# Sixteen sends of rows, two slots apart in GpSimd's order instead of one

## The chip, the cores and the metric

The kernel runs on one core of a Trainium2 chip. The metric is the device time of one execution in microseconds. The time before is the median of three runs, 1697.31 us (1696.88 to 1698.7). The engines are named as the profile names them: PE is TensorE, DVE is VectorE, ACT is ScalarE, POOL is GpSimd, and SP is SyncE, which only issues DMAs here. They run side by side, each through its own instructions in a fixed order, and they meet at semaphores.

## The reference

`x` has the shape 16 x 256 x 512, and so has the context. Four residual steps follow one another; the dimensions are those of the data.

```
x = x + xattn0(layernorm(x), ctx)   # latent attention, norm over the latent, relu, out_w
x = x + ffn0(layernorm(x))          # dense layer plus 2 of 8 low-rank experts per row
x = x + xattn1(layernorm(x), ctx)   # 8 heads, 512 x 512 scores each
x = x + ffn1(layernorm(x))          # 64 experts, top 8 of each row, inner size 192

xattn0: h = relu((t_x - mean) * rsqrt(var + eps) * ln_gamma + ln_beta); out_w @ h + out_b + ctx
ffn1:   probs = softmax(logits); topw, topi = top_k(probs, 8); topw /= sum(topw)
        an expert takes at most CAP rows of each group of 1024, in order of rows
```

Each of the 4096 rows goes to up to eight experts. A row beyond an expert's capacity is dropped for that expert.

## The kernel before, in words

**Stages.** The attention stage works through the 16 batches of 256 rows. It ends with every normalised row copied to the slots of its experts in `slots_dram`, a table in HBM. Then the expert stage reads these slots expert by expert, and the last part merges what two sets of outputs hold.

**Slots.** The attention stage's order is written out by `schedule` (L87). Its unit is the slot, a quarter of a head's 512 x 512 scores: PE multiplies (L691 and L700), DVE takes a maximum (L1209), ACT takes the exponential (L973, `p_t`). A batch has 32 slots. Its preparation (both earlier residual steps) begins 64 slots ahead, and its routing (the `disp` events) follows behind, so at any time several batches are in work. The tables (TENSOR, SCALAR, VECTOR, GPSIMD and their _OUT, _TAIL and _MAX companions) give each step its slot on each engine, and an engine runs its steps sorted by slot. No engine looks at another's order. A step whose input isn't there holds up all that follows on its engine.

**What POOL does per batch.** Counted by the batch's 32 slots, POOL has these steps:

- `add` (L1479): eight sums `p_sum` of two `p_t` tiles, at slots 5 to 8 and 21 to 24. Each needs ACT's `p_t`, and PE sums the result in L727.
- `lat_rstd` (L1451, L1453) at slot 25: the root for the latent norm of a later batch. It waits for DVE's `lat_all` (L1121). DVE's L1126 waits for it, then L1130, then ACT's relu (L917), then PE's `out_w` product (L642).
- `rstd2`, `rstd4` and `rstd` (L1408 to L1416): roots and offsets of the other norms.
- `res0` and `res1` (L1446): the residual additions of the context.
- the dispatch `rstd` (L1408, L1410), at slot 14.25 of the next batch: the root for the rows that are sent.
- `send`, 16 per batch (L1491), from slot 31 of the next batch but one: an indirect DMA that scatters 128 rows of 577 values by the expert slots in `slot_i`. The first waits for `slots_ok`, DVE's last routing step of that batch (L1307), and all wait for the slots to have been filled once with defaults. Each counts up `sent`; DVE's writing of rows two batches later (L1248) waits for that count.

**The lines behind it.** PE's L663 and L656 are the low-rank products of ffn0, read by DVE's `lora_mid` (L1149); L620 is a product of the latent attention, which waits for ACT's `prob` (L907); L723 turns the maxima, read by ACT's `max_hi` (L980) and DVE's `max_lo` (L1218); L753 is the router's product, read by DVE's `r_max` (L1255); L798 is the expert stage's first product.

**The end of the attention stage.** Behind the last batch's additions stand, in POOL's order, the 16 sends of batch 13, then batch 15's dispatch `rstd`, then the 32 sends of batches 14 and 15. The expert stage's first reads (`x_slots<-slot_rows`) wait for all sends.

Of the kernel before, what the change touches and what calls it, by code (L numbers as in the profile page):

```python
# [32 lines left out]
class Count:  # L33
# [5 lines left out]
    def up(self, by=1):  # L39
# [25 lines left out]
SCALAR_OUT = {"x0": 38.25, "x1": 40.25, "exp": 42.5}  # L65
VECTOR_OUT = {"stats0": 10.25, "stats1": 12.75, "rows0": 16.5, "rows1": 17.75, "peak": 42.25, "top0": 43.75,
              "top1": 43.75, "top2": 43.75, "place0": 44.5, "place1": 44.5, "place2": 46.5}
GPSIMD_OUT = {"rstd": 14.25, "send": 63}
SYNC_OUT = {"out": 10}

TENSOR_TAIL = {"sums0": -4, "sums2": -3.5, "sums1": 0.25}
# [15 lines left out]
def schedule(dims, prepare, tail, maxima, dispatch, core):  # L87

    B, HALF, NHEAD, C = dims["B"], dims["HALF"], dims["NHEAD"], dims["T"] // P
    H4 = NHEAD // HALF
    QUAD, SLOTS = C * H4, NHEAD * C
    AHEAD = LEAD * H4
    out = []
    if "fill" in core:
        late = dims["NEXP"] - FIRST_FILLS
        out += [(prepare["k0"] - PREPARE, 0, ("fill", n)) for n in range(FIRST_FILLS)]
        out += [(FILL_FROM + n * FILL_SLOTS / late - PREPARE, 0, ("fill", FIRST_FILLS + n)) for n in range(late)]
    for n in range(B * SLOTS):  # L100
        if "key" in core:
            out.append((n, 0, ("key", n)))
        if "score" in core:
            out.append((n - AHEAD, 1, ("score", n)))
        if "add" in core and n // H4 % C == 1:
            out.append((n + 1, 2, ("add", n)))
        if "weighted" in core and n % H4 == 0:
            out.append((n + WEIGHTED, 2, ("pv", n // H4)))
    for quad in range(B * HALF):
        out += [(QUAD * (quad + 1) - AHEAD - 1 + o, 3, ("tail", quad, what)) for what, o in maxima.items()]  # L110
        out += [(QUAD * (quad + 1) + o, 3, ("tail", quad, what)) for what, o in tail.items()]
    for b in range(B):
        out += [(SLOTS * b - PREPARE + o, 4, ("prep", b, what)) for what, o in prepare.items()]
        for what, o in dispatch.items():
            for n in range(HALF * dims["TOPK"] if what == "send" else 1):
                out.append((SLOTS * (b + 1) + o + n, 5, ("disp", b, what, n)))
    return [(at, ev) for at, _, ev in sorted(out, key=lambda x: x[:2])]


# [20 lines left out]
def build(nc, a, out, out_odd, slots_dram, dims):  # L140
# [22 lines left out]
    BC = NHEAD * C  # L163

    tensor_order = schedule(dims, TENSOR, TENSOR_TAIL, TENSOR_MAX, TENSOR_OUT, ("key", "score", "weighted"))
    scalar_order = schedule(dims, SCALAR, SCALAR_TAIL, SCALAR_MAX, SCALAR_OUT, ("key",))
    vector_order = schedule(dims, VECTOR, VECTOR_TAIL, VECTOR_MAX, VECTOR_OUT, ("score",))
    gpsimd_order = schedule(dims, GPSIMD, {}, {}, GPSIMD_OUT, ("add",))
    sync_order = schedule(dims, SYNC, {}, SYNC_MAX, SYNC_OUT, ("fill",))
# [1428 lines left out]
```

## Time and profile before

| | before |
|---|---|
| median of 3 runs | 1697.31 us |
| profiled execution: span, first to last instruction | 1788.0 us |
| PE busy | 1562.6 us (87%) |
| DVE busy | 1256.5 us (70%) |
| ACT busy | 971.5 us (54%) |
| POOL busy | 807.0 us (45%) |
| sends, L1491 | 256 in POOL, 255.0 us busy |
| additions, L1479 | 128, 168.5 us busy |
| mean granted PE clock | 0.935 |

The profiled execution is one execution with the recording on, and its span is the only time that the profile gives of it; it gives none for what lies around the span. It is 90.7 us above the median of the runs, which were taken without recording. The attention stage fills the span up to 1231.43 us, where PE begins the first expert (L798). The sends stand in it from 289.2 to 1226 us. A share of busy time is an average: in a steady batch PE is nearly always busy, and at the end of the stage POOL alone is.

### The profile page before, as it was taken

What the parts mean: (1) busy time and instruction counts of PE and PEld (TensorE: products, weight loads), DVE (VectorE), ACT (ScalarE), POOL (GpSimd) and SP (SyncE); (2) the same over time, 40 slices, a digit from 0 to 9 for tenths busy, and PEclk for the clock granted to TensorE, in tenths of its full rate; (3) what the DMA queues carried; (4) which work ended last, traced back from release to release, by engine and by line L of the source; (5) the groups of instructions that cost most, each with busy time, mean ns of one, the idle gap of its engine ahead of it and who ended that gap; (6) DMA issues with size and microseconds to landing.
All of it is one profiled execution on the core that took longest, in us unless ns stands there. A gap on an engine that the chain in (4) does not pass through costs nothing.

```text
span 1788.0 us, 25255 instructions
## 1 busy us (share of the span) xinstructions
PE 1562.6 (87%) x8016; PEld 999.9 (56%) x8016; DVE 1256.5 (70%) x2994; ACT 971.5 (54%) x1938; POOL 807.0 (45%) x893
## 2 busy tenths in 40 slices
PE   5799999999999999999899898724999999999980
PEld 2444454454444454444444443324999999999970
DVE  2477778767767677687677676434888888888850
ACT  3355665655655655655656544412666666666640
POOL 4122325454463554464454535654444444444440
PEclk8889999999999999999999998956999999999995
DMA  9968863463463444433422422025999999999969
GB/s 328 309 196 298 270 206 113 132 206 106 132 186 121 128 132 127 135 102 99 134 75 79 113 53 57 23 96 181 287 291 297 297 290 295 297 299 288 296 104 188
DMA packets 156099, 329.22 MB, mean 184 GB/s; under 512 B 28010, under 2 KB 38122, under 8 KB 154944
## 3 DMA queue, kind: packets, MB, share of 16 engines
q1 hardware_dynamic: 115968, 247.80, 42.4%
q0 software_dynamic: 40000, 79.82, 20.4%
q8 instruction: 64, 1.05, 0.2%
q14 instruction: 67, 0.55, 0.1%
HBM read 149.64 MB, written 173.21 MB: 181 GB/s over the span
## 4 chain that ended last, share of the span: by engine, by line
PE 69%; DVE 9%; another core or an unknown queue 5%; issue 4%; SPq 4%; ACT 3%; POOL 2%; DMA 2%; DVEq 1%; POOLq 0%; ACTq 0%
PE bank L700 7%; PE bank L712 6%; PE bank L691 5%; PE bank L809 5%; PE bank L811 5%; PE bank L810 5%; PE bank L798 3%; PE bank L669 3%; PE bank L734 3%; PE bank L614 2%; SPq L492 2%; DVE max_col L1209 2%; PE bank L620 2%; PE bank L832 2%
## 5 line engine op out<-in xcount | busy, mean ns | idle before, releaser
L1209 DVE TENSOR_REDUCE max_col<-bank 128x1 f32<-128x512 f32 x512 | 341.0, 683 | 173.4 <-PE bank L691 155.8
L973 ACT ACTIVATE p_t<-bank 128x512 f32<-128x512 f32 x512 | 294.4, 596 | 217.1 <-PE bank L700 195.3
L1491 POOL DMA_INDIRECT slot_rows<-row,slot_i x256 | 255.0, 996 | 77.6 <-issue 76.9
L700 PE MATMUL bank<-q_stack,k_stack 98*128 98x512 f32 x512 | 278.5, 546 | 8.3 <-DMA q_stack<-max_lo 4.2
L1479 POOL TENSOR_TENSOR p_sum<-p_t 128x512 f32<-128x512 f32 x128 | 168.5, 1322 | 214.1 <-ACT p_t L973 211.5
L691 PE MATMUL bank<-k_stack,q_stack 96*128 96x512 f32 x512 | 214.1, 420 | 4.7 <-DVE max_col L1209 4.4
L700 PEld LDWEIGHTS bank<-q_stack,k_stack 98*128 98x128 f32 x512 | 98.5, 193 | 196.4 <-issue 170.1
L809 PE MATMUL bank<-gate_up_hi,x_slots_t_hi 128*128 128x384 f32 x512 | 183.4, 358 | 0.5 <-DVE x_slots_t_lo L1337 0.5
L1533 POOL DMA_INDIRECT out_rows<-y_slots,row_ids x64 | 110.0, 1719 | 153.9 <-ACT y_slots L1045 150.7
L811 PE MATMUL bank<-gate_up_hi,x_slots_t_lo 128*128 128x384 f32 x512 | 172.4, 337 | 0.0
L810 PE MATMUL bank<-gate_up_lo,x_slots_t_hi 128*128 128x384 f32 x512 | 172.0, 336 | 0.0
L1533 POOL DMA_INDIRECT out_rows_odd<-y_slots,row_ids x64 | 109.6, 1713 | 132.1 <-ACT y_slots L1045 127.9
L712 PE MATMUL bank<-p_t,v_t 128*32 128x512 f32 x1024 | 143.3, 633 | 0.2 <-DVE head_sb L1225 0.2
L1045 ACT ACTIVATE y_slots<-bank,x_slots 128x512 f32<-128x512 f32 x128 | 88.2, 689 | 100.6 <-PE bank L836 100.6
L669 PE MATMUL bank<-base_w,x_t 128*128 128x512 f32 x256 | 132.0, 630 | 0.0
L691 PEld LDWEIGHTS bank<-k_stack,q_stack 96*128 96x128 f32 x512 | 99.9, 195 | 52.8 <-issue 29.1
L1337 DVE TENSOR_TENSOR x_slots_t_lo<-bank,x_slots_t_hi 128x512 fp32r<-128x512 f32 x128 | 88.0, 688 | 54.7 <-ACT x_slots_t_hi L1025 39.5
L1362 DVE TENSOR_TENSOR gate_up_lo<-gate_up,gate_up_hi 128x768 fp32r<-128x768 f32 x128 | 121.7, 951 | 0.0
L1055 ACT CAST gate_up_hi<-gate_up 128x768 fp32r<-128x768 f32 x128 | 105.5, 825 | 10.8 <-DMA gate_up<-in_gate_up 10.8
L798 PE MATMUL bank<-ident,x_slots 128*128 128x128 f32 x512 | 77.4, 274 | 38.3 <-DMA x_slots<-slot_rows 38.3
L1408 POOL TENSOR_SCALAR row_rstd<-row_mv 128x2 f32<-128x2 f32 x48 | 11.0, 228 | 205.2 <-DVE row_mv L1095 205.2
L809 PEld LDWEIGHTS bank<-gate_up_hi,x_slots_t_hi 128*128 128x128 f32 x512 | 96.9, 189 | 1.1 <-DVE x_slots_t_lo L1337 0.9
(188 smaller groups left out, 3296.4 us busy)
## 6 DMA issues: line engine op xcount, KB each, us to landing
gate_up<-in_gate_up SPq DMA_DIRECT2D x64, 768.0 KB
slot_rows<-row SPq DMA_DIRECT2D x64, 577.0 KB, 8.2
x_slots<-slot_rows SPq DMA_DIRECT2D x64, 577.0 KB, 5.7
k_stack<-prob SPq DMA_DIRECT2D x192, 128.0 KB, 3.8
down<-in_down SPq DMA_DIRECT2D x64, 384.0 KB, 8.9
q_stack<-x_t SPq DMA_DIRECT2D x128, 128.0 KB
out_rows_odd<-row SPq DMA_DIRECT2D x17, 512.0 KB, 5.5
x<-in_x SPq DMA_DIRECT2D x16, 512.0 KB, 3.3
```

Of the source, the lines that this page charges most:

```text
L669: e.matmul(bank[:, :], x_t[:, k, c, :], base_w[:, c, :], start=c == 0, stop=False)
L691: e.matmul(psum[2 + n % 2][:, :], q_st[b % 2][0:SK, head, c * P:(c + 1) * P], k_st[b % 2][0:SK, head, :], start=True, stop=True).then_inc( ...
L700: e.matmul(psum[n % 2][:, :], k_st[b % 2][0:SKM, head, j * P:(j + 1) * P], q_st[b % 2][0:SKM, head, :], start=True, stop=True).then_inc(fu ...
L712: m = e.matmul(psum[4][h * DQ:(h + 1) * DQ, :], v_t[b % 2][:, j, head + h, :], p_t[step % 2][:, h, :], start=j == 0, stop=j == C - 1)
L809: e.matmul(bk[:, 0:2 * INNER], xt_hi[u % 3][:, c, :], gu_hi[nw][:, c, :], start=c == 0, stop=False)
L810: e.matmul(bk[:, 0:2 * INNER], xt_hi[u % 3][:, c, :], gu_lo[nw][:, c, :], start=False, stop=False)
L811: m = e.matmul(bk[:, 0:2 * INNER], xt_lo[u % 3][:, c, :], gu_hi[nw][:, c, :], start=False, stop=c == C - 1)
L973: e.activation(p_t[step % 2][:, h, :], psum[n % 2][:, :], ACT.Exp, scale=SCALE).then_inc(free[n % 2], 1)
L1209: e.tensor_reduce(max_col[quad % 2][:, h, c:c + 1], psum[2 + n % 2][:, :], X, ALU.max, negate=True).then_inc(free[2 + n % 2], 1)
L1479: e.tensor_tensor(p_sum[:, h, :], p_t[(step - 1) % 2][:, h, :], p_t[step % 2][:, h, :], ALU.add).then_inc(p_sum_ok, 1)
L1491: e.indirect_dma_start(out=slots_dram, in_=rows[b % 2][:, k, :], in_offset=None, out_offset=bass.IndirectOffsetOnAxis(ap=slot_i[b % 2][:, ...
L1533: e.indirect_dma_start(out=out_odd if e_ % 2 else out, out_offset=bass.IndirectOffsetOnAxis(ap=row_ids[e_ % NI][:, q, :].bitcast(U32), axi ...
```

## The change

The first send of a batch moves from slot 63 of the dispatch table to slot 48, and the 16 sends stand two slots apart. The last stays where it was: 63 + 15 = 48 + 2 x 15 = 78. Counted by the 32 slots of a batch, the sends of batch b stood at 31 of batch b+2 and 0 to 14 of batch b+3; now they stand at 16, 18, ... 30 and 0, 2, ... 14. Nothing else is changed. The orders of PE, DVE, ACT and SP are the same as before, and so are the semaphores and their counts.

```diff
-GPSIMD_OUT = {"rstd": 14.25, "send": 63}
+GPSIMD_OUT = {"rstd": 14.25, "send": 48}
+SEND_STEP = 2
...
             for n in range(HALF * dims["TOPK"] if what == "send" else 1):
-                out.append((SLOTS * (b + 1) + o + n, 5, ("disp", b, what, n)))
+                out.append((SLOTS * (b + 1) + o + n * SEND_STEP, 5, ("disp", b, what, n)))
```

Line numbers behind the new line are one higher after: the send is L1491 before and L1492 after.

POOL in a steady batch, from slot 21 on, before. `p_sum` is the addition, `lat_all` is `lat_rstd`, `row_rstd` and `row_off` here are `rstd2`, `slot_rows` is a send:

```order
L1479 TENSOR_TENSOR p_sum<-p_t 128x512 x4
L1451 TENSOR_SCALAR lat_all<-lat_all 128x1
L1453 TENSOR_TENSOR lat_all<-lat_all,neg_half 128x1
L1408 TENSOR_SCALAR row_rstd<-row_mv 128x2
L1410 TENSOR_TENSOR row_rstd<-row_rstd,neg_half 128x2
L1414 TENSOR_TENSOR row_off<-row_mv,row_rstd 128x2
L1416 TENSOR_SCALAR row_off<-row_off 128x2
```

POOL at the same place after. Three sends and two additions stand where the four additions began:

```order
L1492 DMA slot_rows<-row,slot_i 16384x577 x3
L1480 TENSOR_TENSOR p_sum<-p_t 128x512 x2
L1492 DMA slot_rows<-row,slot_i 16384x577
L1480 TENSOR_TENSOR p_sum<-p_t 128x512 x2
L1492 DMA slot_rows<-row,slot_i 16384x577
L1452 TENSOR_SCALAR lat_all<-lat_all 128x1
L1454 TENSOR_TENSOR lat_all<-lat_all,neg_half 128x1
L1492 DMA slot_rows<-row,slot_i 16384x577 x2
L1409 TENSOR_SCALAR row_rstd<-row_mv 128x2
```

Three sends (slots 16, 18 and 20) now stand ahead of the additions of slots 21 to 24, one stands in the middle of these four and one between the last of them and `lat_rstd`, and two (slots 26 and 28) stand between `lat_rstd` and `rstd2`.

POOL at the end of the attention stage before, from the last four additions on. The 16 sends are batch 13's, the 32 are those of batches 14 and 15, and `row_rstd` is batch 15's dispatch `rstd`:

```order
L1479 TENSOR_TENSOR p_sum<-p_t 128x512 x4
L1491 DMA slot_rows<-row,slot_i 16384x577 x16
L1408 TENSOR_SCALAR row_rstd<-row_mv 128x2
L1410 TENSOR_TENSOR row_rstd<-row_rstd,neg_half 128x2
L1491 DMA slot_rows<-row,slot_i 16384x577 x32
```

POOL there after:

```order
L1492 DMA slot_rows<-row,slot_i 16384x577 x3
L1480 TENSOR_TENSOR p_sum<-p_t 128x512 x2
L1492 DMA slot_rows<-row,slot_i 16384x577
L1480 TENSOR_TENSOR p_sum<-p_t 128x512 x2
L1492 DMA slot_rows<-row,slot_i 16384x577 x12
L1409 TENSOR_SCALAR row_rstd<-row_mv 128x2
L1411 TENSOR_TENSOR row_rstd<-row_rstd,neg_half 128x2
L1492 DMA slot_rows<-row,slot_i 16384x577 x32
```

Four sends moved from behind the four last additions to places ahead of and between them; the 32 at the end are as before.

## Rows read from the trace of the kernel before

**Rows 1.** The page: span; the chain that ended last, by engine.
```profile
span 1788.0 us, 25255 instructions
...
PE 69%; DVE 9%; another core or an unknown queue 5%; issue 4%; SPq 4%; ACT 3%; POOL 2%; DMA 2%; DVEq 1%; POOLq 0%; ACTq 0%
```

**Rows 2.** Windows: A:B, us, then each engine's busy time (instructions), PEclk, DMA share, GB/s.
```profile
215.10:277.50 62.40, 62.06 (x318) 31.78 (x318) 50.23 (x128) 40.46 (x82) 19.12 (x27) 1.00 0.63 198
...
343.60:1039.20 695.60, 647.20 (x3170) 328.59 (x3170) 509.73 (x1271) 403.86 (x811) 351.32 (x421) 0.97 0.40 121
```

**Rows 3.** Waits of PE, 290 to 1130 us: total us, times, longest.
```profile
PE bank L663 <- DVE gated L1187: 26.3, 12, 3.8
...
PE bank L620 <- ACT prob L907: 25.8, 11, 3.0
```

**Rows 4.** Waits of ACT, 290 to 1130 us.
```profile
ACT max_hi L980 <- remote: 33.1, 11, 3.6
```

**Rows 5.** Timeline, 946 to 950 us: start, us, engine, line, operation, [idle before <-releaser].
```profile
946.35 0.28 PE L723 MATMUL bank<-ident,max_col 128*16 128x128 f32 x1
...
946.38 0.97 POOL L1491 DMA_INDIRECT slot_rows<-row,slot_i  x1 [0.30 <-issue]
...
948.97 0.25 ACT L980 CAST max_hi<-bank 16x128 fp32r<-16x128 f32 x1 [2.68 <-remote]
```

**Rows 6.** Chain of waits, 1140 to 1240 us: start, us, what.
```profile
1162.96 12.79 another core or an unknown queue
```

**Rows 7.** All sends, line L1491: duration min/median/max in ns.
```profile
L1491 POOL DMA_INDIRECT slot_rows<-row,slot_i x256: 967/973/1371, 289.2 to 1225.2; - x128
```

**Rows 8.** L1451 (lat_rstd) on POOL: ns min/median/max, first and last; what it waited for.
```profile
L1451 POOL TENSOR_SCALAR lat_all<-lat_all x16: 185/190/192, 31.2 to 1040.8; 128x1 f32<-128x1 f32 x16
...
  DVE lat_all L1121: 45.0, 16
```

**Rows 9.** Timeline of POOL, 894 to 909 us.
```profile
894.26 2.62 POOL L1479 TENSOR_TENSOR p_sum<-p_t 128x512 f32<-128x512 f32 x2 [10.60 <-ACT p_t L973]
...
897.21 2.60 POOL L1479 TENSOR_TENSOR p_sum<-p_t 128x512 f32<-128x512 f32 x2 [0.32 <-ACT p_t L973]
...
900.43 0.19 POOL L1451 TENSOR_SCALAR lat_all<-lat_all 128x1 f32<-128x1 f32 x1 [0.63 <-DVE lat_all L1121]
...
900.71 0.56 POOL L1453 TENSOR_TENSOR lat_all<-lat_all,neg_half 128x1 f32<-128x1 f32 x1
...
908.38 0.22 POOL L1408 TENSOR_SCALAR row_rstd<-row_mv 128x2 f32<-128x2 f32 x1 [7.11 <-DVE row_mv L1095]
```

**Rows 10.** Timeline of DVE, `slots_ok` of the batch that is sent next.
```profile
885.08 0.17 DVE L1307 TENSOR_SCALAR slot_i<-slot 128x16 int32<-128x16 f32 x1
```

**Rows 11.** Timeline of DVE, ACT and PE, 901 to 906 us.
```profile
901.46 0.74 DVE L1126 SCALAR_TENSOR_TENSOR theta<-theta,lat_all,ln_gamma 128x512 f32<-128x512 f32 x1
...
903.02 0.63 ACT L917 ACTIVATE theta<-theta 128x512 f32<-128x512 f32 x1
...
903.86 1.98 PE L642 MATMUL bank<-theta,out_w 128*128 128x512 f32 x4
```

**Rows 12.** Timeline of POOL, a send between two additions, 1122 to 1125 us.
```profile
1122.85 0.99 POOL L1491 DMA_INDIRECT slot_rows<-row,slot_i  x1 [0.16 <-issue]
...
1123.86 1.30 POOL L1479 TENSOR_TENSOR p_sum<-p_t 128x512 f32<-128x512 f32 x1
```

**Rows 13.** Timeline of POOL, last additions to last sends, 1147 to 1184 us.
```profile
1147.66 4.99 POOL L1479 TENSOR_TENSOR p_sum<-p_t 128x512 f32<-128x512 f32 x4 [7.65 <-ACT p_t L973]
...
1172.07 0.97 POOL L1491 DMA_INDIRECT slot_rows<-row,slot_i  x1 [0.30 <-issue]
...
1181.38 0.22 POOL L1408 TENSOR_SCALAR row_rstd<-row_mv 128x2 f32<-128x2 f32 x1 [8.33 <-DVE row_mv L1095]
...
1183.17 1.29 POOL L1491 DMA_INDIRECT slot_rows<-row,slot_i  x1 [0.76 <-DVE slot_i L1307]
```

**Rows 14.** Timeline of DVE, the last routing step.
```profile
1175.78 0.29 DVE L1255 TENSOR_REDUCE r_max<-bank 128x2 f32<-128x128 f32 x1 [12.82 <-remote]
```

## The prediction

> **What bounds the kernel now.** I read the page first, with the times beside it. The span is 1788.0 us [rows 1], and the median of the runs is 1697.31 us: the recorded execution is 90.7 us longer. Then I read where the chain of waits goes. PE has 69% of it, and 5%, some 89 us, is put down to "another core or an unknown queue" [rows 1]. There is no other core here, so the reader should see time for which no instruction of the kernel accounts. The windows tell where it lies. A batch before the first send takes 62.40 us, of which PE is busy 62.06. Ten batches with sends take 695.60 us, 69.56 each, with 64.72 busy [rows 2]. The 7.16 us per batch are what such waits make: in 12 batches PE waits 26.3 us for `gated` and 25.8 us for `prob` [rows 3], and ACT's `max_hi` sits 33.1 us behind nothing that is shown, 11 times [rows 4]. One of these: PE's L723 has begun at 946.35 and takes 0.28 us, ACT's L980, which waits for it alone, begins at 948.97, 2.68 us idle, while sends run back to back from 946.38 [rows 5]. The largest is 12.79 us, in the run of 16 sends at the end [rows 6].
>
> Two readings are possible: the sends hold up the signals between engines in every execution, or only while a record is taken. By the first, the runs of 1697.31 us contain the 89 us; by the second they don't. I take the second, because of a sum. The excess of the recorded execution over the timed ones (90.7) is the size of the unexplained part of the chain (89); if the timed runs contained it too, the 90.7 us would need another source, and I found none. With the stalls gone, a batch of the timed run is the 62.4 us of the first window: PE is busy for 99% of it, and any delay that PE meets stays. That holds from about 215 to 1130 us. From there on POOL is the bound: its sends follow one another and the expert stage waits for the last.
>
> The Trainium skill bears on this ("NOTIFIC — the notification-queue block", 7.1 Overflow): the path that carries records pushes back inside rather than lose one. By that rule the recording can throttle an engine, and the gaps here would be its doing; the page gives no time for it. The trace agrees as far as a gap of 2.68 us stands under back-to-back sends, but cannot prove it.
>
> **The change, part by part.** It adds and removes no instruction; 256 sends of 973 ns (median; 967 to 1371) stay [rows 7]. Only their places in POOL's order move. All is worked out for the batch at 894 us. There are 12 like it: `lat_rstd` stands in batches -2 to 13 by POOL's order, 64 slots ahead of its own, the sends stand in batches 2 to 17, and 2 to 13 have both.
>
> *Three sends ahead of the additions* (slots 16, 18, 20). They wait for `slots_ok`, here 885.08 + 0.17 = 885.25 [rows 10]. Three sends at a pitch of 1.28 us (0.97 + 0.30) end at 889.1. The additions begin at 894.26 after 10.60 us of idleness [rows 9]. The idle time hides them: nothing, with 5.2 us to spare; were `slots_ok` that much late, additions and PE's L727 would be late by the rest.
>
> *Two sends among the additions and `lat_rstd`* (22 and 24). This is the term that decides. Before, the additions are 894.26 + 2.62 = 896.88, then 897.21 + 2.60 = 899.81 with an idle 0.32, and `lat_rstd` begins at 900.43, 0.63 us after POOL is free, when DVE's value is there [rows 9]. It waits for DVE in all 16 batches, 45.0 us together [rows 8], and the last of them is at 1040.8 us. It ends at 900.71 + 0.56 = 901.27, and DVE's L1126 begins at 901.46 [rows 11]: 0.19 us of slack. A send between two additions costs 1.17 us (1122.85, next addition 1123.86, and 0.16 idle before) [rows 12]. So after: additions to 896.88, send to 898.05, additions to 900.65, send to 901.82, `lat_rstd` until 902.66. L1126 then begins 1.2 us late. Behind it on DVE stand L1130, `max_col` and all else. ACT's relu stood at 903.02, 0.63 long, and PE's L642 at 903.86 [rows 11], 0.21 us behind it. So PE is held 1.0 to 1.2 us. PE is at 99% in such a batch [rows 2], so no later idleness takes this up: 12 x 1.1 = 13 us. Bounds: 0 if DVE catches up before PE needs it; 12 x 1.5 = 18 if neither the 0.32 us of idleness between the additions nor the 0.19 us of slack is there without recording.
>
> *Two sends behind `lat_rstd`* (26, 28). They end by 902.66 + 2.6 = 905.3; `rstd2` begins at 908.38 after 7.11 us of idleness [rows 9]. Hidden, with 3 us to spare.
>
> *The other nine* (30, and 0 to 14 by twos). Before, all 16 stood in slots 31 to 14; there are fewer now, so `rstd4`, the residual additions and the additions of slots 5 to 8 come no later. Gain: nothing in a steady batch, because PE doesn't wait for these in the first window either. Bounds: 0 to -0.3 us a batch.
>
> *The end.* Four of batch 13's 16 sends go from behind the last additions to before and between them. Before, the four additions run from 1147.66 to 1152.65 and the sends until 1172.07 + 0.97 = 1173.04. Then the dispatch `rstd` waited 8.33 us for DVE, until 1181.38, and the 32 sends begin at 1183.17 [rows 13]. DVE was late by the 12.79 us of rows 6: its `r_max` began only at 1175.78 [rows 14], 5.60 us ahead of `rstd`. Without the stall DVE would allow `rstd` at 1181.38 - 12.79 = 1168.6, and POOL is the bound, until 1173.04. After, three sends (3.8 us) fit into the 7.65 us of idleness ahead of the additions [rows 13], one among them costs 1.17, and 12 follow: 1152.65 + 1.17 + 12 x 1.28 = 1169.2. That is 3.8 us sooner and close to what DVE allows. I take -3, bounds -4 and 0 (if DVE's chain is late for another reason). In the two groups of additions before these a send costs or gives at most 1.5 us; I take 0.
>
> Sum: 13 - 3 = 10 us. Its terms are from the profiled execution, cleared of the stalls; since the runs are taken to be without them, it is added to their median: 1697.31 + 10 = 1707 us. The span of the recorded execution is a different sum: of its 89 us of stalls most would go, because sends in runs of four and fewer take the place of runs of six to eight, so it should fall: 1788 - 0.8 x 89 + 13 = 1730 us or a little more, although the time rises.
>
> **Rivals.**
>
> *A, the stalls are in the timed runs too.* Then spreading the sends removes most of 7.16 us in ten batches, say nine tenths, 65 us, less the 13 of `lat_rstd`: 52 us faster, 1645 us. For it speaks that the gaps stand exactly where sends are dense; against it, the 90.7 us that the recorded execution is longer. Chance 0.12.
>
> *B, DVE's delay doesn't reach PE.* For it: DVE is busy only 50.23 of 62.40 us [rows 2], so it recovers within microseconds. Against it: the relu's end (903.02 + 0.63) and L642 are 0.21 us apart [rows 11], so PE is there before DVE has recovered. Then the sum is between -3 and +3, within 1697.3 +- 3.4. Two tenths of a per cent, 3.4 us, is about what a measurement of this kernel can tell from no change. Chance 0.11.
>
> *C, the delay costs more than itself.* DVE's `max_col` behind L1126 frees PE's banks; 1.2 us late there and 1.2 us late at relu might add instead of overlap, as both engines restart behind PE: up to 12 x 1.8 = 22 less 3, 1716 us. For it: DVE waits for PE's L691 and PE for DVE's `max_col` by turns in every slot; against it, the banks give them a slot or more of play. Chance 0.17.
>
> *D, the order doesn't matter in the timed run*, because without stalls ACT's `p_t` comes sooner than in the trace and POOL's work slides apart. The slack of `lat_rstd` is the same in all batches, so I give it no more than 0.02, inside B's time.
>
> **How the numbers follow.** Forecast 0.58 (1701 to 1713), A 0.12, B and D 0.13, C 0.17. The predicted time is the likeliest, 1707. The range leaves out A, which lies 45 us off, and little else: 1693 to 1716. Slower by over 0.2%: forecast and C, 0.75. Within: 0.11 of B and D. Faster: A and the edge of B, 0.14.
>
> **What would show it.** In the profile after, POOL's `lat_all` L1452 should no longer wait for DVE in those 12 batches, and DVE's L1127 should wait for POOL 1.2 us in 12 batches, PE's L643 for ACT's relu 1 us. The "unknown queue" share should drop under 2%, with a span of 1730 to 1740. Batch 15's dispatch `rstd` should wait for POOL's sends less than before. The forecast is wrong if the time falls with the span (A), or if DVE's L1127 waits 12 times and PE doesn't (B).

## The result, and the profile after

| | before | after |
|---|---|---|
| median, measured side by side, 12 runs each | 1698.09 us (1694.62 to 1705.42) | 1706.51 us (1704.65 to 1708.6) |
| ratio, 95% interval | | 1.0046 [1.0034, 1.0058] |
| profiled execution: span | 1788.0 us | 1703.0 us |
| mean granted PE clock | 0.935 | 0.955 |
| POOL busy | 807.0 us | 819.6 us |

The changed kernel is 8.4 us slower. Its profiled execution took 1705.14 us, so 2.1 us lie around its span. That is within the range of its timed runs; the 1788.0 us of the kernel before lie far above the range of its own.

The page of the changed kernel, its span and the chain by engine, is the counterpart of [rows 1]:

```profile
span 1703.0 us, 25255 instructions
...
PE 33%; POOL 2%; issue 2%; DVE 2%; DMA 1%; ACT 1%; POOLq 0%; DVEq 0%; SPq 0%; ACTq 0%
```

The "unknown queue" is gone from the chain. The first window (columns as in [rows 2]) holds ten batches with sends, the second one earlier batch, in which only the first three sends stand:

```profile
338.50:977.70 639.20, 620.60 (x3171) 317.86 (x3171) 510.64 (x1271) 406.57 (x811) 361.62 (x421) 1.00 0.44 130
...
212.10:274.60 62.50, 62.10 (x318) 31.83 (x318) 50.48 (x128) 40.54 (x82) 22.58 (x30) 1.00 0.67 213
```

A batch with sends takes 63.92 us, the one before them 62.50. The 69.56 us and the PE clock of 0.97 of [rows 2] don't come back. The 1.4 us more per batch show as two waits, PE's and then DVE's (total us, times, longest; 290 to 1130 us):

```profile
PE bank L724 <- DVE max_col L1210: 16.9, 11, 1.6
```

```profile
DVE theta L1127 <- POOL lat_all L1454: 9.8, 11, 0.9
```

Neither wait was there before. PE's two waits of [rows 3], for `gated` and `prob`, are gone (one of 0.6 us is left for `gated`). Before, POOL was free early at `lat_rstd` and waited for DVE's value in all 16 batches [rows 8]. Now it waits only in four:

```profile
L1452 POOL TENSOR_SCALAR lat_all<-lat_all x16: 185/188/193, 31.0 to 980.9; 128x1 f32<-128x1 f32 x16
...
  DVE lat_all L1122: 35.9, 4
```

One batch on POOL, the counterpart of [rows 9]. The send that was put between the additions, and the one behind them:

```profile
845.15 2.62 POOL L1480 TENSOR_TENSOR p_sum<-p_t 128x512 f32<-128x512 f32 x2 [3.28 <-ACT p_t L974]
847.92 1.27 POOL L1492 DMA_INDIRECT slot_rows<-row,slot_i  x1
849.21 2.52 POOL L1480 TENSOR_TENSOR p_sum<-p_t 128x512 f32<-128x512 f32 x2
851.89 0.99 POOL L1492 DMA_INDIRECT slot_rows<-row,slot_i  x1 [0.17 <-issue]
852.96 0.19 POOL L1452 TENSOR_SCALAR lat_all<-lat_all 128x1 f32<-128x1 f32 x1
853.23 0.58 POOL L1454 TENSOR_TENSOR lat_all<-lat_all,neg_half 128x1 f32<-128x1 f32 x1
```

`lat_rstd` comes 0.1 us behind a send, with no idle time. DVE, ACT and PE there (before: [rows 11]), from PE's L635 on, from whose result DVE makes its value:

```profile
849.79 0.38 PE L635 MATMUL bank<-lat_mv,ones 128*128 128x2 f32 x2 [0.32 <-DVE lat_mv L1118]
...
851.01 0.74 DVE L1122 SCALAR_TENSOR_TENSOR lat_all<-lat_all 128x1 f32<-128x1 f32 x1
...
853.84 0.75 DVE L1127 SCALAR_TENSOR_TENSOR theta<-theta,lat_all,ln_gamma 128x512 f32<-128x512 f32 x1 [0.89 <-POOL lat_all L1454]
...
855.42 0.63 ACT L918 ACTIVATE theta<-theta 128x512 f32<-128x512 f32 x1 [1.41 <-DVE theta L1131]
...
856.13 0.27 PE L724 MATMUL bank<-ident,max_col 128*16 128x128 f32 x1 [1.56 <-DVE max_col L1210]
```

Read them in time. L1127 waits 0.89 us for POOL, ACT's relu waits 1.41 for DVE, and PE's L724, which stands ahead of L643, waits 1.56 us for the `max_col` that DVE does behind L1131. The row 851.01 is a second matter: L1122 took 0.22 us in the kernel before, in the row that follows, and takes 0.74 here.

```profile
900.13 0.22 DVE L1121 SCALAR_TENSOR_TENSOR lat_all<-lat_all 128x1 f32<-128x1 f32 x1
```

The end on POOL (before: [rows 13]), from the first of the 12 sends behind the last additions to the first of the 32:

```profile
1080.01 0.99 POOL L1492 DMA_INDIRECT slot_rows<-row,slot_i  x1 [0.17 <-issue]
...
1094.11 0.98 POOL L1492 DMA_INDIRECT slot_rows<-row,slot_i  x1 [0.30 <-issue]
...
1096.39 0.22 POOL L1409 TENSOR_SCALAR row_rstd<-row_mv 128x2 f32<-128x2 f32 x1 [1.30 <-DVE row_mv L1096]
...
1098.19 1.29 POOL L1492 DMA_INDIRECT slot_rows<-row,slot_i  x1 [0.75 <-DVE slot_i L1308]
```

The 12 sends take 15.1 us, and `rstd` then waits 1.30 us for DVE where it waited 8.33. PE's first product of the experts:

```profile
1146.55 1.94 PE L799 MATMUL bank<-ident,x_slots 128*128 128x128 f32 x8 [38.41 <-DMA x_slots<-slot_rows]
```

The span ends 556.5 us behind it, as before (1231.43 + 556.6). So the whole difference of the spans lies ahead of the experts.

### The profile page after: what moved, and what is told of

Its sections match the earlier page's. It is cut to its first block and busy times, and to the rows that moved or that the text cites. A ratio compares the mean times of both kernels' runs of the same rounds, so it can differ in the third digit from the quotient of the medians.

```text
span 1703.0 us, 25255 instructions
## 1 busy us (share of the span) xinstructions
PE 1525.4 (90%) x8016; PEld 983.2 (58%) x8016; DVE 1258.4 (74%) x2994; ACT 974.0 (57%) x1938; POOL 819.6 (48%) x893
## 5 line engine op out<-in xcount | busy, mean ns | idle before, releaser
L1492 POOL DMA_INDIRECT slot_rows<-row,slot_i x256 | 266.6, 1041 | 104.0 <-issue 68.6
L713 PE MATMUL bank<-p_t,v_t 128*32 128x512 f32 x1024 | 137.2, 608 | 0.2 <-DVE head_sb L1226 0.2
L670 PE MATMUL bank<-base_w,x_t 128*128 128x512 f32 x256 | 124.6, 599 | 0.0
L811 PEld LDWEIGHTS bank<-gate_up_lo,x_slots_t_hi 128*128 128x128 f32 x512 | 97.1, 190 | 0.0
```

Of the source, the lines that this page charges most:

```text
L713: m = e.matmul(psum[4][h * DQ:(h + 1) * DQ, :], v_t[b % 2][:, j, head + h, :], p_t[step % 2][:, h, :], start=j == 0, stop=j == C - 1)
L811: e.matmul(bk[:, 0:2 * INNER], xt_hi[u % 3][:, c, :], gu_lo[nw][:, c, :], start=False, stop=False)
L1492: e.indirect_dma_start(out=slots_dram, in_=rows[b % 2][:, k, :], in_offset=None, out_offset=bass.IndirectOffsetOnAxis(ap=slot_i[b % 2][:, ...
```

## The experiments

The kernel before ran beside each group, and it took 1794.63, 1793.4, 1772.14 and 1785.38 us in these four, not 1698. So in these groups its timed runs are as long as its first profile was. The groups ran on chips 8, 4, 12 and 12; which chip the first measurement used isn't known. The kernels are therefore compared within a group, or by the length of a batch in their profiles. That length is here the distance from the fifth to the last of DVE's 16 `lat_stat` (L1115 before), divided by 11.

| kernel | time, us | ratio to the kernel before | batch, us | last `lat_stat` to first expert, us |
|---|---|---|---|---|
| before, first profile | (1698.09) | | 69.25 | 193.1 |
| after, first profile | (1706.51) | 1.0046 | 63.92 | 169.8 |
| e1 before again | 1792.41 | 0.9994 [0.9964, 1.0025] | 69.29 | 194.1 |
| e2 `lat_rstd` ahead | 1708.48 | 0.9523 [0.9493, 0.9553] | 63.17 | 180.8 |
| e3 steady only | 1726.12 | 0.9617 [0.9591, 0.9643] | 64.18 | 184.6 |
| e4 tail only | 1792.35 | 0.9983 [0.9953, 1.0014] | 69.28 | 191.9 |
| e5 after again | 1724.26 | 0.9626 [0.9595, 0.9657] | 64.22 | 179.6 |
| e6 none among | 1710.85 | 0.9550 [0.9520, 0.9580] | 62.66 | 181.0 |
| e7 one ahead | 1712.68 | 0.9673 [0.9588, 0.9758] | 63.15 | 179.9 |
| e8 old tail | 1710.12 | 0.9674 [0.9586, 0.9762] | 62.64 | 184.1 |
| e9 run of six | 1721.88 | 0.9733 [0.9648, 0.9818] | 63.70 | 182.7 |
| e10 half rows | 1793.36 | 1.0145 [1.0056, 1.0235] | 69.47 | 189.6 |
| e11 paced | 1740.01 | 0.9728 [0.9684, 0.9772] | 64.45 | 193.4 |
| e12 none among again | 1709.54 | 0.9571 [0.9525, 0.9617] | 62.71 | 180.6 |

Groups: e1 to e4, e5 and e6, e7 to e10, e11 and e12. Each profile is one execution. In what follows, a stall is time in which an engine sits idle though the profile shows nothing that it still waits for ("remote" or "another core or an unknown queue").

**e1, the kernel before once more** (no edit).

> The kernel before, unchanged, recorded once more. Theory (the stalls belong to the recording): time within 0.2% of the kernel before; if this recorded execution again has stalls, its span is up to 90 us above its timed runs and its batches with sends take 66 to 72 us; if it has none, its span is about 2 us under its time and its batches are constant, 62.4 to 63.0 us long. Rival (the stalls are in every execution): the batches take about 69.6 us and the timed runs sum up to that.

```profile
span 1792.0 us, 25255 instructions
...
PE 69%; DVE 9%; another core or an unknown queue 4%; issue 4%; SPq 4%; ACT 3%; POOL 2%; DMA 2%; ACTq 0%; POOLq 0%; DVEq 0%
```

Its time is that of the kernel before in the same group, 1794.63, but 94 us above the 1698.09 of the first measurement. Its ACT waits as [rows 4] shows, here over the whole span:

```profile
ACT max_hi L980 <- remote: 27.7, 10, 3.9
```

The span of each timed run here is some 2.1 us under its time, so timed runs are this long too, not only the profile. That doesn't settle the prediction's question. Every one of these timed runs, and of the kernel before in all four groups, carries a span and a clock, so something was recorded in each. Leaving out one of 2261.82 us, they take 1758 to 1805 us. Its 12 runs of the first measurement, for which no span is listed, take 1695 to 1705. So the two readings, stalls only under recording and stalls in some measurements, are not told apart by this kernel. The changed kernel adds one thing: its first profile is a recorded execution, with 12 and 32 sends in a row at its end, and shows no stall, where every other profile here has some at its end. Recording alone is then not enough. Whether it is needed, and whether the chip matters, is open.

**e5, the changed kernel once more** (no edit).

> The changed kernel once more, beside the kernel before on the same chip. If the chip makes the difference, the kernel before takes either 1698 or 1794 us here. Theory (dense sends stall the other engines only in some executions, and spaced sends don't): the changed kernel takes 1705 to 1715 us in both cases; so it is 8 us slower where the kernel before takes 1698, and 85 us faster where it takes 1794. Rival (everything is slower on such a chip): it takes 1790 us or more there.

The changed kernel takes 1724.26 us where the kernel before takes 1793.4: 69 us faster, 3.7%. Of the 18 us over the first measurement, 3.3 are in the batches (11 x 0.3, 64.22 against 63.92), 4.9 lie ahead of the fifth `lat_stat`, where no send stands yet, and 9.8 at the end, where 12 and 32 sends still stand in a row: 179.6 against 169.8 us. One piece of its chain of waits there:

```profile
1098.53 2.88 another core or an unknown queue
```

So one kernel pair gives two results: 8 us slower in the first measurement, and 69 us faster in a group where runs of sends stall the others.

**e2, `lat_rstd` ahead of the second send.**

```diff
-GPSIMD = {..., "lat_rstd": 25, ...}
+GPSIMD = {..., "lat_rstd": 24, ...}
```

> The changed kernel with lat_rstd at slot 24 instead of 25, so that it stands behind the addition of slot 24 and ahead of the send of slot 24; all sends stay two slots apart. Theory (the loss is lat_rstd held up by two sends): one of the two is out of its way, DVE's wait for lat_all falls from 0.9 us a batch to about 0 to 0.2, PE's wait at L724 from 1.5 to 0.3 us or less, the batch from 63.9 to 62.5 us or so, the time to 1689 to 1693 us, under the kernel before. Rival (the loss comes from the send between the additions or from elsewhere): 1705 us as after. Rival (only one send's 1.2 us is recovered, but PE waits for max_col anyway): 1698 us.

The batch falls from 64.18 us (e3, same group, same steady part as the changed kernel) to 63.17: 1.0 us, not the 1.4 of the theory. DVE's wait for `lat_all` is gone but for one batch. PE's wait at L724 is a third of what it was, and longer than the 0.3 us a batch expected:

```profile
PE bank L724 <- DVE max_col L1210: 5.0, 9, 0.6
```

What is left is in DVE's row 848.72. L1122 is still stretched to 0.74 us, because the send between the additions has pushed the last addition over it, and PE waits 0.55:

```profile
848.72 0.74 DVE L1122 SCALAR_TENSOR_TENSOR lat_all<-lat_all 128x1 f32<-128x1 f32 x1
...
850.59 0.74 DVE L1127 SCALAR_TENSOR_TENSOR theta<-theta,lat_all,ln_gamma 128x512 f32<-128x512 f32 x1
...
852.86 0.27 PE L724 MATMUL bank<-ident,max_col 128*16 128x128 f32 x1 [0.55 <-DVE max_col L1210]
```

**e6 and e12, no send among the additions.**

```diff
-SEND_STEP = 2
+SENDS = (48, 49, 50, 51, 58, 59, 60, 62) + tuple(range(64, 80, 2))
...
-                out.append((SLOTS * (b + 1) + o + n * SEND_STEP, 5, ("disp", b, what, n)))
+                out.append((SLOTS * (b + 1) + o + (SENDS[n] - 48 if what == "send" else 0), 5, ("disp", b, what, n)))
```

> The changed kernel with other places for eight of its sends: none stands among the additions of slots 21 to 24 or ahead of lat_rstd behind them. Sends at 16, 17, 18, 19, 26, 27, 28, 30 and 0, 2, ... 14; never more than four in a row. Theory: DVE's wait for lat_all is 0, a batch takes 62.4 to 62.9 us, 1.1 to 1.5 less than in the changed kernel, the time is 13 to 17 us lower than the changed kernel's in the same call, about 1690. Rival (a run of four or a send behind the additions costs as much): within 3 us of the changed kernel.

> The kernel with none among the additions once more, beside the kernel before. Theory: 1705 to 1712 us where the kernel before takes 1770 to 1795; about 1690 where it takes 1698 (the changed kernel's 1706.5 less 12 x 1.3).

The batch is 62.66 us, 1.56 less than in e5, and the time 13.4 us less (1724.26 to 1710.85, one group). In the two profiles the spans are 17.2 apart (1721.5 and 1704.3): eleven batches at 1.56 make 17.2, and 1.4 more at the end are made up ahead of the fifth batch. The medians are 13.4 apart; the e6 profile is the fastest of its five runs. The window of ten batches, columns as in [rows 2]:

```profile
339.70:966.60 626.90, 621.98 (x3172) 318.62 (x3170) 505.43 (x1272) 405.19 (x811) 354.75 (x421) 1.00 0.45 132
```

PE is busy for 99.2% of them. The same edit again, e12, gives 1709.54 us. This version beats the kernel before in both groups and the changed one in the one that they share. It was not measured where the kernel before takes 1698 us, so that it would win there is not shown. The changed kernel's 1706.51 less 13.4 would be 1693 us there, an estimate.

The same places as in the profile after, in e6:

```profile
842.14 0.38 PE L635 MATMUL bank<-lat_mv,ones 128*128 128x2 f32 x2 [0.32 <-DVE lat_mv L1118]
...
843.36 0.22 DVE L1122 SCALAR_TENSOR_TENSOR lat_all<-lat_all 128x1 f32<-128x1 f32 x1
...
844.70 0.74 DVE L1127 SCALAR_TENSOR_TENSOR theta<-theta,lat_all,ln_gamma 128x512 f32<-128x512 f32 x1
```

L1127 begins 2.56 us behind L635; in the changed kernel it was 4.05. L1122's durations (min/median/max in ns) show the second price by itself. First before (there L1121):

```profile
L1121 DVE SCALAR_TENSOR_TENSOR lat_all<-lat_all x16: 219/219/221, 30.8 to 1040.5; 128x1 f32<-128x1 f32 x16
```

after:

```profile
L1122 DVE SCALAR_TENSOR_TENSOR lat_all<-lat_all x16: 219/741/750, 30.6 to 978.9; 128x1 f32<-128x1 f32 x16
```

and e6:

```profile
L1122 DVE SCALAR_TENSOR_TENSOR lat_all<-lat_all x16: 219/220/221, 29.9 to 968.7; 128x1 f32<-128x1 f32 x16
```

**e7, one send ahead of `lat_rstd`, none between the additions** (`SENDS` with 56 in place of 51).

> As the kernel with none among the additions (16 to 19, 26, 27, 28, 30, 0 to 14), but one send moves from slot 19 to slot 24, between the last addition of slots 21 to 24 and lat_rstd. Theory (lat_rstd has 0.63 us of idleness ahead and 0.19 us of slack behind it, and a send there costs 1.15 to 1.2): DVE's L1127 comes 0.35 us late, a batch takes 62.95 to 63.1 us against 62.65 there, the total is 4 to 5 us above that kernel. Rival (a send costs its full 1.2 us): 63.8 us a batch, +14. Rival (hidden): within 2.

DVE waits 0.37 us a batch, what is left of one send (1.17) after the 0.63 us of idleness and the 0.19 us of slack ahead of it:

```profile
DVE theta L1127 <- POOL lat_all L1454: 4.1, 11, 0.4
```

The batch is 63.15 us, 0.5 longer than e8's and e6's. The time was to be 4 to 5 us above e6's, which didn't run in this group; it is 2.6 above e8's. The send between the additions alone (e2) costs 0.5 too, and the pair 1.56: more than the two apart, since the slack can be used only once.

**e3 and e4, the steady batches and the end apart.** e3 sends as in the changed kernel up to batch 12 and as before from 13 on; e4 the other way round (`> 12`).

```diff
+def send_at(b, n):
+    return n * SEND_STEP if b <= 12 else 15 + n
...
```

> Batches 0 to 12 send as in the changed kernel, 13 to 15 as before. Theory: the whole loss of the steady batches stays and the end's gain goes: the kernel before + 12 x 1.1 to 1.5 = 1711 to 1716 us. If the end's gain is nothing, 1706 as after.

> Batches 0 to 12 send as before, 13 to 15 as in the changed kernel. Theory: only the end's gain: 3 us by the prediction, up to 8 by the difference between 12 batches x 1.5 us and the measured 8.4: 1690 to 1695 us. Rival (the end gains nothing, a steady batch loses 0.7 us): 1698 us. Together with the run that changes the steady batches alone the differences should sum to that of the whole change, +8.4 us.

The absolute forecasts of e2, e3 and e4 fell with the 1698 us they started from. e4 is inconclusive: 2.3 us under the kernel before, with an interval that holds zero. The two differences, 68.5 and 2.3 us, sum to 70.8, close to the 69 us of the whole change in e5. For the end the profiles tell more, with one execution each. In this group the changed end is 3.8 us shorter than the old one (e2 180.8, e3 184.6), and 2.2 shorter in the orders with long runs (e4 191.9, e1 194.1). e3 and e5, of two groups, differ only in the end: 5.0 us.

**e8, the old end under the version e6** (batches 13 to 15 send at slot 31 and 0 to 14).

> The kernel with none among the additions for batches 0 to 12, the sends of 13 to 15 as in the kernel before (slot 31 and 0 to 14). Theory: it costs what the changed end gains, 3 to 5 us by POOL's order (four sends of 1.28 us less behind the last additions), and by the stalls of a run of 16 in place of 12 perhaps 2 to 5 more where runs are stalled: 1713 to 1719 us. Rival (the end gains 10 us, the whole difference between 12 x 1.5 and the measured 8.4): 1720 or more.

The time is 3 us under the forecast, and within 1 us of e6's and e12's, which ran in other groups. In the profiles the end is 184.1 us, against 179.9 in e7 of the same group and 181.0 and 180.6 in e6 and e12: the changed end gains 3.1 to 4.2. All comparisons together give 2 to 5 us, and all of them have stalls in them.

**e9, six sends in a row in place of four** (the other line as in e6).

```diff
-SEND_STEP = 2
+SENDS = (48, 49, 50, 51, 58, 59, 60, 61, 62, 64, 66, 67, 68, 74, 76, 78)
```

> The kernel with none among the additions, with six sends in a row between rstd2 and the next addition in place of four, and the others moved to match. Where dense sends stall the other engines from about the fifth of a run: a batch takes 1.5 to 3 us longer, in all 20 to 35 us more than the kernel with runs of at most four. Where there are no such stalls: the same time within 2 us. Rival (the stalls come from how many sends a batch has, not from runs): the same in both.

The batch grows from 62.64 (e8, same group) to 63.70 us, and the time from 1710.12 to 1721.88. PE's wait for `gated`, absent in e8 but for 0.6 us, is back, 1.1 us a batch:

```profile
PE bank L664 <- DVE gated L1188: 13.0, 12, 2.0
```

The number of sends is the same, so the price comes from how they stand. It was about half of what I expected: 1.06 us a batch, not 1.5 to 3, and 11.8 us in all, not 20 to 35. Two sends moved, from slots 6 and 8 to 29 and 3. None of PE's waits from 290 to 1030 us is for POOL, but a way over ACT's wait for POOL's `x_off` (26.5 us, in e8 23.5) isn't excluded.

**e10, half of each send's rows.** The kernel before, with 64 of the 128 rows per send; rows 64 to 127 are left out.

```diff
-                        out=slots_dram, in_=rows[b % 2][:, k, :], in_offset=None,
+                        out=slots_dram, in_=rows[b % 2][0:64, k, :], in_offset=None,
```

(and `slot_i` cut alike.)

> The kernel before with sends of 64 of the 128 rows each; the other half of the rows is left out. Theory (the stalls follow the amount of row transfers in a run of sends): they vanish or shrink to a fifth, and the time is 1690 to 1710 us where the kernel before takes 1794. Rival (they follow the number of sends): 1780 to 1795 us. In the latter case the recorded batches stay at 66 to 72 us.

The theory that I had written down falls. The packets of POOL's queue, which also carries the output rows of the expert stage, fall from 40000 to 31808:

```profile
q0 software_dynamic: 31808, 61.50, 19.3%
```

yet the batch stays at 69.47 us and ACT's `max_hi` still sits idle 33 us behind nothing:

```profile
ACT max_hi L980 <- remote: 32.7, 11, 3.2
```

The stalls don't shrink with the rows that a send moves. The time is 21 us above the kernel before in its group (1772.14), at the upper end of the rival's 1780 to 1795.

**e11, a pause behind every second send.**

```diff
+        pace = A("pace", [P, 512])
...
+                    if b <= 12 and n % 2:
+                        e.memset(pace[:, :], 0.0).then_inc(pool_step, 1)
+                        w.wait_ge(pool_step, step.up())
```

> The kernel before, and behind every second send of batches 0 to 12 POOL clears an unused 128 x 512 tile, some 0.5 to 0.8 us. So POOL has more work, but its sends no longer follow one another at 1.28 us for more than two. Theory (the stalls come from runs of sends, each at 1.28 us): batches fall from about 69 to 64 to 66 us, the time by 40 us or more against the kernel before in the same call, though POOL does 5 us more per batch. Rival (what helped in the changed kernel was not the distance between sends): no change, or slower by the added work: DVE waits for POOL's dispatch rstd.

POOL does 57.3 us more, and the kernel is 45.4 us faster than the kernel before in its group. The places of the sends in the order are the old ones. The groups of operations on POOL:

```profile
L1492 POOL DMA_INDIRECT slot_rows<-row,slot_i x256 | 259.2, 1012 | 103.4 <-issue 79.1 <-POOL pace L1497 23.4 <-DVE slot_i L1308 0.8
...
L1497 POOL MEMSET pace<- 128x512 f32 x104 | 57.3, 551 | 0.1
```

A batch takes 64.45 us, where both profiles of the kernel before have 69.3. PE's wait for `gated`, first in e1 and then here (290 to 1030 us in both):

```profile
PE bank L663 <- DVE gated L1187: 25.7, 11, 2.8
...
PE bank L664 <- DVE gated L1188: 7.8, 8, 2.5
```

This and e9 show from two sides that, where stalls appear, what decides is how many sends follow one another without a pause.

## Why the prediction was right

**The time.** 1707 us was forecast and 1706.51 measured. The direction and the place of the loss were right for the reason given. That the number fits to 0.5 us is luck: the median that it was added to is 0.8 us higher in the full measurement, the main part was too small by 4 to 6 us, and something that the forecast doesn't have makes up for it.

**Two sends among the additions and `lat_rstd`: right in kind and place, somewhat too small.** L1127 was to come 1.2 us late in 12 batches. The profile after shows the wait (11.8 us in 13 batches, one of them in the kernel before too), and e2, e6 and e7 show that moving either send takes part of it away. Counted from PE's L635, L1127 begins 4.05 us later (849.79, 853.84), against 2.56 in e6 (842.14, 844.70): 1.49 us late, not 1.2. The step's rows 12 gave a send among the additions 1.17 us; here it took 1.27 alone (847.92) and 1.44 with what lies around it. The term was to be 12 x 1.1 = 13. It is 12 x 1.42 = 17 by the first profile (63.92 - 62.50 a batch), and 12 x 1.56 = 19 by e5 and e6, on either side of the upper bound of 18. The wait that was forecast for PE, at L643 for ACT's relu, isn't there in these batches. PE is held one step ahead of it, at L724, by the `max_col` that DVE does behind L1131.

**What that step didn't see.** A later addition lies over L1122, which then takes 741 ns in place of 219. Here it hides under the wait for `lat_rstd`. Where that wait is taken away (e2), it is the 0.5 us that stay. The Trainium skill has the rule ("SBUF — State Buffer", "Who interferes with whom"): a DVE instruction with two SBUF inputs contends with a GpSimd instruction that reads SBUF. L1122 takes two, the addition reads two, and the traces agree: in the changed kernel's two profiles, in e2's and in e3's an addition stands beside it in 12 batches each and it takes 735 to 752 ns, and 219 to 220 or 221 in the other four. In e7 a send stands beside it in 12 batches, and it takes 219 to 221.

**What was called hidden was hidden.** The three sends ahead of the additions begin at 838.25 and are done at 841.9; the additions wait for ACT until 845.15. The two behind `lat_rstd` end at 856.8; POOL then idles 3.97 us up to `rstd2` at 860.77. Among DVE's waits from 290 to 1130 us none is for a send.

**The end: the size fits as far as it was measured.** -3 was forecast, with bounds of -4 and 0. The profiles with stalls give -2 to -5. Without stalls only the changed end was recorded (169.8 us), so its gain there isn't measured.

**Where the two parts meet.** 17 to 19 less 2 to 5 is 12 to 17 us, and the measured difference is 8.4 (5.8 to 9.9 by its interval). So in the first measurement the kernel before must lose 2 to 11 us that the changed one doesn't, beside the 62.4 us that I took for its batches. No execution of it without stalls was recorded, so where these lie, in its batches or in its end, stays open. Its 12 runs spread over 10.8 us and those of the changed kernel over 4.0, which would fit leftovers of the stalls, but doesn't show it.

**The stalls: the choice was right for the measurement, its reason is not confirmed.** I chose "only while a record is taken" over "in every execution". "In every execution" is wrong: the first 12 runs, of 1698 us, are 94 us shorter than the stalled ones and have no room for them. "While a record is taken" isn't the whole of it either: the changed kernel's first profile has a record, 44 sends at its end and no stall. But a part of the recording is not excluded: all runs of the kernel before that carry a span (1758 to 1805 us) are long. Nor is the chip excluded: the later groups ran on three chips and the first measurement's isn't known. Where stalls appear, runs of sends cost from 1.1 us a batch (six in a row, e9) up to 7 (the old order). That the first runs of the kernel before were taken without recording, as said above beside its first profile, is an assumption: no span is listed for them, and no more is known. The rule of the Trainium skill that was weighed there ("NOTIFIC — the notification-queue block", 7.1 Overflow) is neither borne out nor refuted by these runs. Rival A, 52 us faster, was given 0.12: its direction is what e5 measured, with 69 us, and 0.12 was little for a mechanism whose absence rested on one subtraction. (A's 1645 us lie 48 us below the range, not the 45 that the prediction names.) The recorded span fell to 1703, further than the 1730 or 1740 forecast: no stall was left in it, where a fifth was to stay.

**The other rivals.** B, that the delay doesn't reach PE: PE waits 16.9 us at L724 in 11 batches, so it fell. C, that it costs more than the 1.1 us a batch: by 0.3 to 0.5, of the 0.7 that it assumed, and PE does wait for the `max_col` that C names. But two delays that add aren't needed for it, since L1127 alone is 1.49 us late. D, that order doesn't matter in the timed run, fell with e2 and e6.

## What to carry to other kernels

Before an instruction is put into a gap of a busy engine's order, count what comes behind the gap: the slack of the next instruction that another engine waits for pays once, for the first one. Spread transfers into stretches where their engine idles, not evenly over the slots: here the same 16 sends cost 1.4 to 1.6 us a batch more when two of them stand among the additions than when none does, and the batch with none there (62.66 us) is within 0.3 of one before the sends (62.40 to 62.50). When a recorded execution is 5% longer than the timed ones, find out which of the two a later measurement resembles before resting an argument on either.

## What the runs showed of the hardware

- While POOL issues six or more scattering DMAs in a row, one every 1.28 us, other engines can stand idle with nothing shown that they wait for: ACT up to 3.9 us (e1). The idle time didn't shrink when each DMA moved half the rows (e10). A 551 ns clearing behind every second send took most of it away in the steady batches (e11). Six in a row cost 1.06 us a batch more than four (e9 against e8), and runs of at most four cost 0.3 or less (64.22 against 63.92).
- It is not there in every measurement. The old order took 1698 us in one and 1772 to 1795 in four others. The spaced order took 1706.5 and 1724 us. What decides between them, the recording, the chip or something else, isn't shown.
- A DVE operation of one column with two inputs, 219 ns, takes 741 ns (median) when a POOL addition of 128 x 512 runs beside it (after), and still 219 when a send does (e7).
